# Top-k attention on one NeuronCore: row maximum and hand-on values computed ahead of a flag's load and branch

## The reference, cut to what matters

```python
scores = jnp.einsum('bhnd,bhmd->bhnm', q, k) * DHEAD ** (-0.5)
kth = jax.lax.top_k(scores, TOPK)[0][..., -1:]
masked = jnp.where(scores >= kth, scores, jnp.finfo(scores.dtype).min)
attn = jax.nn.softmax(masked, axis=-1)
o = jnp.einsum('bhnm,bhmd->bhnd', attn, v)
```

## Time and profile before

| | us |
|---|---|
| median of 3 runs | 5124.61 |
| lowest, highest | 5120.05, 5127.47 |
| the profiled execution, its own time | 5125.56 |
| its span in the trace | 5123.8 |
| DVE busy / ACT busy / PE busy | 4325.4 / 4155.0 / 4131.7 |

### The profile page before, as it was taken

One profiled execution on the slowest core, in us unless ns is written; L12 is line 12 of the kernel. 1 busy time (PEld: TensorE's weight loads), 2 busy tenths in 40 slices (PEclk: granted clock), 3 DMA queues, 4 the chain that ended last, 5 costly groups with the idle time before them and its releaser, 6 DMA issues. The chain is left out here.

```text
span 5123.8 us, 106951 instructions
## 1 busy us (share of the span) xinstructions
PE 4131.7 (81%) x32161; PEld 2787.5 (54%) x32161; DVE 4325.4 (84%) x25276; ACT 4155.0 (81%) x6082; POOL 1502.6 (29%) x362
## 2 busy tenths in 40 slices
PE   8577677776777677767777767899899999999999
PEld 4354444444444444544454444443567777777776
DVE  4999999999999999999999999430368888888886
ACT  2799799998999789989999899644268888888885
POOL 0344445544454444444444444200100000000000
PEclk9677777777777777777777777899799999999999
DMA  6000000000000000000000000200330111111112
GB/s 214 7 18 17 8 17 17 8 17 15 11 17 17 7 17 8 18 16 8 18 18 8 17 17 8 67 6 0 133 93 25 34 25 34 25 34 32 27 34 94
DMA packets 79597, 154.62 MB, mean 30 GB/s; under 512 B 8120, under 2 KB 49464, under 8 KB 73528
## 3 DMA queue, kind: packets, MB, share of 16 engines
q1 hardware_dynamic: 78904, 146.72, 10.1%
HBM read 99.50 MB, written 47.19 MB: 29 GB/s over the span
## 5 line engine op out<-in xcount | busy, mean ns | idle before, releaser
L542 POOL TENSOR_TENSOR a_probs<-a_scores,a_probs 128x2304 f32<-128x2304 f32 x288 | 1460.7, 5093 | 1671.3 <-ACT a_probs L465 1671.3
L560 DVE MAX8 a_top<-a_scores 128x8 f32<-128x36 f32 x18432 | 1831.6, 180 | 57.4 <-ACT a_scores L449 45.9
L376 PE MATMUL a_ps_t<-ident,a_probs 128*128 128x128 f32 x5184 | 965.2, 323 | 594.4 <-ACT a_probs_t L460 458.0
L376 PEld LDWEIGHTS a_ps_t<-ident,a_probs 128*128 128x128 f32 x5184 | 665.8, 162 | 884.4 <-ACT a_probs_t L460 597.8
L465 ACT ACTIVATE a_probs<-a_scores,a_steep_kth 128x2304 f32<-128x2304 f32 x290 | 641.2, 2211 | 183.5 <-DVE a_minus_max L692 183.5
L1292 DVE TENSOR_SCALAR_CACHE_REDUCE b_soft<-b_ps_s 128x2304 f32<-128x2304 f32 x288 | 735.0, 2552 | 26.5 <-PE b_ps_s L1151 8.5
L460 ACT ACTIVATE a_probs_t<-a_ps_t 128x512 f32<-128x512 f32 (+1 forms) x1440 | 725.8, 545 | 18.4 <-PE a_ps_t L376 6.2
L1167 PE MATMUL b_ps_t<-ident,b_soft 128*128 128x128 f32 x5184 | 727.0, 276 | 1.6 <-DVE b_soft_t L1298 0.6
L1167 PEld LDWEIGHTS b_ps_t<-ident,b_soft 128*128 128x128 f32 x5184 | 578.5, 140 | 170.3 <-ACT b_soft_t L1256 60.1
L453 ACT ACTIVATE a_probs<-a_probs,a_minus_max 128x2304 f32<-128x2304 f32 x288 | 637.9, 2215 | 30.5 <-issue 18.5
L366 PE MATMUL a_ps_s<-a_k_stack,a_q_ring 128*128 128x512 f32 (+1 forms) x1465 | 647.3, 601 | 15.9 <-ACT a_scores L449 11.1
(11 more groups left out here) (133 smaller groups left out, 4138.6 us busy)
## 6 DMA issues: line engine op xcount, KB each, us to landing
a_k_stack<-k_parts SPq DMA_DIRECT2D x72, 288.0 KB, 6.0
b_k_stack<-k_parts SPq DMA_DIRECT2D x72, 288.0 KB, 6.0
a_q_ring<-q_parts SPq DMA_DIRECT2D x294, 64.0 KB
b_q_ring<-q_parts SPq DMA_DIRECT2D x294, 64.0 KB
k_parts<-p_high SPq DMA_DIRECT2D x36, 256.0 KB, 2.1
k_parts<-p_rest SPq DMA_DIRECT2D x36, 256.0 KB, 2.1
q_parts<-p_high SPq DMA_DIRECT2D x36, 256.0 KB, 2.0
q_parts<-p_rest SPq DMA_DIRECT2D x36, 256.0 KB, 2.0
```

Of the source, the lines that this page charges most:

```text
L376: last = pe.transpose(ps_t[(NTG * s + g) % 2][:, P * m:P * m + P], probs[s % 2][:, P * (m0 + m):P * (m0 + m) + P], cst["ident"][:, :])
L542: pool.tensor_tensor(probs[u][:, :], scores_all[:, 2 * (p % 2) + u, :], probs[u][:, :], ALU.subtract).then_inc(masked_ready, 1)
L560: last = dve.max(top8[s // 2 % 2][:, s % 2, c, :], scores_all[:, s % 4, CHUNK * c:CHUNK * c + CHUNK])
```

## The change

- `prepare` loses the tensor_reduce over both tiles. In its place each tile gets a second max instruction over the chunks' eighth places, into the new tile `eighths`. `select` reads `eighths` where it read `extremes`.
- `hand_on` now starts, after the clearing of `dve_order`, with a tensor_reduce that takes the row's maximum of both tiles (`first_of_row`), then `steep_kth`, then a wait on the new semaphore `first_ready` (incremented by the tensor_reduce) and `minus_max`, which increments `kth_ready`. Only then come the wait for `any_ready`, the load of the flag and the branch. Inside the branch `search_again` is followed by `steep_kth` once more and by drains. Behind the branch stands an increment of the new semaphore `kth_checked`.
- ACT waits for `kth_ready` and then for `kth_checked` ahead of the penalty.

```diff
@@ prepare
-                wait_alone(dve, tops_taken, 2 * pair + 1)
-                counted(dve.max(tops[:, 0, CHUNKS:CHUNKS + REST, 0], tops[:, 0, 0:CHUNKS, KEEP:8]))
-                wait_alone(dve, tops_taken, 2 * pair + 2)
-                counted(dve.max(tops[:, 1, CHUNKS:CHUNKS + REST, 0], tops[:, 1, 0:CHUNKS, KEEP:8]))
-                counted(dve.tensor_reduce(extremes[:, :, :], tops[:, :, 0:CHUNKS, 0:8:7].rearrange("p u c k -> p u k c"),
-                                          AX.X, ALU.max))
+                for u in range(2):
+                    wait_alone(dve, tops_taken, 2 * pair + u + 1)
+                    counted(dve.max(tops[:, u, CHUNKS:CHUNKS + REST, 0], tops[:, u, 0:CHUNKS, KEEP:8]))
+                    counted(dve.max(eighths[:, u, :], tops[:, u, 0:CHUNKS, 7]))
@@ hand_on
-            def give_kth(parity):
-                dve.tensor_scalar(steep_kth[parity][:, :], kth[:, :], STEEP, None, ALU.mult)
-                dve.tensor_scalar(minus_max[parity][:, :], extremes[:, :, 0], -SCALE, None,
-                                  ALU.mult).then_inc(kth_ready, 1)
-
-            def load_doubt(pair):
+            def steepen(parity):
+                return dve.tensor_scalar(steep_kth[parity][:, :], kth[:, :], STEEP, None, ALU.mult)
+
+            def hand_on(pair, parity):
                 after(at["n"])
                 dve.sem_clear(dve_order)
                 at["n"] = 0
+                dve.tensor_reduce(first_of_row[:, :], top8[parity][:, :, 0:CHUNKS, 0], AX.X,
+                                  ALU.max).then_inc(first_ready, 1)
+                steepen(parity)
+                dve.wait_ge(first_ready, pair + 1)
+                dve.tensor_scalar(minus_max[parity][:, :], first_of_row[:, :], -SCALE, None,
+                                  ALU.mult).then_inc(kth_ready, 1)
                 wait_alone(dve, any_ready, pair + 1)
-                return dve.value_load(any_doubt[0:1, 2:3])
-
-            def hand_on(pair, parity):
-                with dve.If(load_doubt(pair) > 0):
+                with dve.If(dve.value_load(any_doubt[0:1, 2:3]) > 0):
+                    dve.drain()
                     search_again(parity)
-                give_kth(parity)
+                    steepen(parity)
+                    dve.drain()
+                dve.sem_inc(kth_checked, 1)
@@ scalar
                     act.wait_ge(kth_ready, pair + 2)
+                    act.wait_ge(kth_checked, pair + 2)
                     penalty(0, 1 - parity)
```

More of the change, by code:

```diff
@@ L297, in attention_top @@
         places, picked = sb("places", [P, WINDOW]), sb("picked", [P, 2, WINDOW])
-        extremes, beyond = sb("extremes", [P, 2, 2]), sb("beyond", [P, 2])
+        first_of_row, eighths, beyond = sb("first_of_row", [P, 2]), sb("eighths", [P, 2, 8]), sb("beyond", [P, 2])
         doubt = sb("doubt", [P, 2])
@@ L317, in attention_top @@
         doubt_ready, doubt_counted, any_ready = sem("doubt_ready"), sem("doubt_counted"), sem("any_ready")
-        kth_ready = sem("kth_ready")
+        first_ready, kth_ready, kth_checked = sem("first_ready"), sem("kth_ready"), sem("kth_checked")
         penalty_ready, masked_ready, probs_ready = sem("penalty_ready"), sem("masked_ready"), sem("probs_ready")
@@ L498, in _ @@
             act.wait_ge(kth_ready, 1)
+            act.wait_ge(kth_checked, 1)
             for u in range(2):
@@ L593, in select @@
                                                      ALU.add, accum_out=above_guess[:, u:u + 1]))
-                counted(dve.tensor_tensor(beyond[:, :], extremes[:, :, 1], tops[:, :, CHUNKS + REST - 1, 0], ALU.max))
+                counted(dve.tensor_tensor(beyond[:, :], eighths[:, :, 0], tops[:, :, CHUNKS + REST - 1, 0], ALU.max))
                 after(rows)
```

## The result

The changed kernel takes 5206.12 us (median of 6 runs, 5204.83 to 5207.60), the kernel before 5125.85 in the same job (6 runs, 5120.05 to 5127.47): a ratio of 1.0159, 95% interval 1.0146 to 1.0172. It is 80 us slower where 95 were forecast, inside the range. The profiled execution of after has a span of 5203.6 us.

A forecast was written before the change was run, and what follows sets the result against it. The prediction took DVE and ACT, waiting for each other in the top-k stage, to bound the kernel. It added 144 x 0.65 + 17 x 0.1 = 95 us to 5125.6, less 1: 5220 us, range 5170 to 5255.

The forecast's parts named there:

- The mechanism: In `hand_on`, `minus_max` waiting for the tensor_reduce holds DVE's sequencer, so load, branch and increment come later: penalty 0.65 us later.
- theory S: The prediction's claim, as the experiments name it: waiting `minus_max` holds DVE's sequencer, load to increment start afterwards; serial load 0.85.
- The load runs alongside: Rival at waiting `minus_max`: DVE's sequencer passes it, penalty 0.20 us earlier in 122 of 144 pairs, 5101 us; chance 0.12.
- The sum of a common pair: Chunk 19 to penalty in the pair traced: penalty at 1661.31 in place of 1660.66, 0.65 us later.
- The register operation: Between `minus_max` and the wait for `any_ready`: 0.04 us, with gaps 0.10 (bounds 0.04 and 0.15).
- The prices of the strided instructions: In `hand_on` and `prepare`: 3.2 ns an element over 0.143 fixed; new tensor_reduce 374 ns, second max 258 ns.
- the low case: Price rival in `hand_on`: tensor_reduce at 0.217 and register operation at 0.04, delay 0.43 us, 5189 us; no separate chance.
- Both paths are 0.3 shorter, so the difference is the same: Pairs whose branch target comes sooner and ACT does not wait, at most 21: the same delay as common pairs.
- The 17 with a search: Searching pairs: load late by the same amount, opening drain 0.1 us at most, behind the search level; 17 x 0.1.
- DVE's restart and prepare: Chunk 20 0.82 us later, `prepare` 0.16 shorter: DVE 0.66 later, level with ACT's scores; nothing counted for the penalty.
- The turn: Penalty to penalty in the top-k stage: 20.53 us before; 21.2 if the forecast is right, 20.3 if wrong.
- The ring: Top-k stage: ACT's penalty waits for DVE's `minus_max`, DVE's first max for ACT's `keep_scores`; a penalty delay delays everything.

The follow-up runs named there:

- experiment 2: Changed kernel with the wait for `first_ready` and `minus_max` moved behind the branch, ACT waiting for `kth_ready` alone: 5119.38 us, 0.9991 of the kernel before.
- (3): Changed kernel with the wait for `any_ready` and the flag's load moved ahead of the waiting `minus_max`, the branch left behind it: 5145.80 us, 1.0042 of the kernel before.
- experiment 5: Changed kernel with only its tensor_reduce issued twelve chunks earlier, behind `select`: 5117.07 us, 0.9980 of the kernel before.
- (7): Changed kernel with a second, identical tensor_reduce into an unused tile ahead of the real one: 5251.90 us, 1.0244 of the kernel before.
- experiment 1: Kernel before with `steep_kth` and `minus_max` ahead of the load and the increment behind the branch, `prepare` and `extremes` unchanged: 5120.73 us, ratio 0.9990.
- 6: Changed kernel with tensor_reduce, `steep_kth`, the wait and `minus_max` all moved up behind `select`: 5119.98 us, 0.9990 of the kernel before.

## Why the prediction was right, and where its sum was off

**The mechanism** is that of the forecast, and three experiments show it from different sides: the waiting `minus_max` moved behind the branch (2), the load moved ahead of it (3), and its wait made to end early (5) each remove the loss, or the part of it that theory S gives to that part; lengthening the wait (7) lengthens the turn by as much. "The load runs alongside" is refuted by the load's start at 1657.8, after `minus_max` at 1657.67, when the flag had been there since 1656.89. In all 144 pairs of the trace the wait for `any_ready` is passed 0.01 to 0.07 us behind the start of `minus_max`, never before it. It was the rival that the Trainium skill favoured ("Perfetto Trace Analysis", Per-engine timelines, which draws the sequencer as free for the next instruction before the semaphores are satisfied); these rows of DVE disagree with the page.

**The sum of a common pair.** Count from the end of chunk 19. Forecast: penalty 1661.31 - 1659.84 = 1.47 us behind it, 0.82 before. Measured: 1658.78 - (1656.09 + 1.26) = 1.43. By its terms: the tensor_reduce starts 0.08 us ahead of that end, as forecast, and `minus_max` starts 0.32 behind it (0.33 forecast). **The register operation was mis-sized**: with its gaps it was put at 0.10 us in the chain, with 0.04 as the lower bound. It isn't in the chain at all. Both waits are for the same value, `pair + 1`, and the one register operation of this stretch now stands on the line of the first of them, L705, ahead of the waiting `minus_max`; in no pair is there another between `minus_max` and the load. Its row in DVE's sequencer in the kernel after, 1656 to 1657.2 us, has it at 1656.4, beside the chunks:

```profile
L705 DVEq ALU_OP  x1: 40/40/40, 1656.4 to 1656.4; - x1
```

The next step of the chain, the wait for `any_ready` (L76), stands 0.015 us behind the start of `minus_max`, in place of 0.10. From there to the first instruction behind the branch it takes 0.98 (0.96 forecast), and from the start of the increment to the penalty 0.11 (0.08 forecast). Together 0.04 less than forecast; that is 0.61 us later than before, where 0.65 was forecast.

**The prices of the strided instructions** came out on wrong counts. The forecast gives the old tensor_reduce 144 elements, the new one 72 and the second max 36. A tile has 64 chunks, and by the shapes in the rows they read 256, 128 and 64. So an element at this stride costs (606 - 143)/256 = 1.8 ns, not 3.2. The three counts are wrong by the same factor, which cancels in 374 and 258: that these two came out is luck. It does not cancel in the lower bounds. 128 contiguous elements take 0.274 us, not 0.217, so the low case would have been 0.06 us a pair higher, some 5197 in place of 5189.

**The pairs in which ACT did not wait.** "Both paths are 0.3 shorter, so the difference is the same" was wrong. The jump between 1678.80 and 1679.58 in DVE's rows above is a short one, and ACT waits 0.59 there. In most pairs with a short jump ACT was not waiting before (in 21 of 28, of which the earlier trace rows shows one), so the first part of the delay only brought DVE level with it. Averaged over the common turns that end in a short jump, 22 before and 16 after and for the most part other pairs, the turn went from 20.51 to 20.83 us, by 0.32; over those with a long one, 97 and 103 turns, from 20.57 to 21.16, by 0.59 (the last of the 120 turns has no branch).

**The sum over the stage.** The 120 common turns are 65 us longer (120 x 0.65 = 78 forecast). The 17 with a search are 14.6 us longer, where 17 x (0.65 + 0.1) = 12.8 were forecast, and the other seven 2.8 (7 x 0.65 = 4.6 forecast). In a search the opening drain costs next to nothing here, since the load comes late anyway, and the closing one 0.17 us, which the forecast had put at level; the sequencer of the kernel after, whole span:

```profile
L710 DVEq DRAIN  x17: 17/17/17, 180.4 to 3084.7; - x17
...
L713 DVEq DRAIN  x17: 167/167/175, 193.8 to 3092.1; - x17
```

Together 83 us from the first penalty to the last, and 80 in the spans. The 13 us that the common turns fall short of the forecast make up nearly all of the miss. By estimate from the numbers above, 120 x 0.04 = 5 of them are the chain without the register operation, and 16 x (0.61 - 0.32) = 5 the short-jump pairs; the rest was not followed up.

**DVE's restart and prepare** were costed at nothing for the penalty, and were: DVE idles 0.94 us behind `minus_max` (about 1.0 forecast) and still waits for ACT's scores 139 times. **The turn** was forecast at 21.2 and is 1658.78 - 1637.54 = 21.24 in the pair shown, 21.14 at the median of all turns.

**In the experiments** the sizes of three gains were missed (1, 5 and 6). The expectations of 1 and 5 let nearly all of ACT's wait turn into a shorter ring. In 1 the other engine of the ring had only 0.18 us in reserve, which bounds the gain but does not by itself explain why it was 0.05; in 5 the searching pairs took half back. What held back 6 stays open. The ring has little to give at this place at all: ACT's wait in the common turns, 0.26 us at the mean before, is 31 us over 120 turns.

## What to carry to other kernels

On DVE here, a wait in front of a cheap instruction was paid by the control instructions queued behind it: a load, a branch and an increment, most of which until then ran for free beside other work. Before putting work ahead of such a chain, look for what in it waits, and give the producer a distance of its own, as experiment 5 did with the same tensor_reduce. And when one engine of a ring is made earlier, look at the reserve of the other: the idle time in front of its first instruction of a turn bounds what the ring can gain as long as the other engine's own path stays as it is. That bound is argued, not shown; in experiment 1 the gain was 0.05 us with a reserve of 0.18.

## What the runs showed of the hardware that was not expected

- DVE's sequencer runs past instructions that only wait for the engine (in experiment 2 the load starts at 1616.1, the tensor_reduce issued ahead of it at 1616.30), but not past one that waits for a semaphore, even if the tensor_reduce that it waits for takes only 0.36 us (after: load at 1657.8, behind `minus_max` at 1657.67).
- The cost of the control behind a branch that is not hidden: load 0.30 us, branch 0.07, and 0.47 more until the first instruction behind a long jump (means over the turns of after; 0.15 for a short one). Why some pairs get the short jump was not tried.
- A drain on DVE took 17 ns where the instructions issued ahead of it had long ended (opening drain, after), and 247 at the median where some of them had yet to run (experiment 5); there it ended some 0.05 us behind the reported end of the last of them.
